# At most two row transfers in flight, and first batch of eight tiles, in a routed-experts kernel

## The reference, cut to what matters

```python
x = x + L0_ffn(L0_cond(x))
X = L1_cond(x)                                   # (64 sequences, 64, 256)
X = X + attention(rmsnorm(X, g1))                # the "block"
xf = rmsnorm(X, g2).reshape(-1, 256)             # 4096 tokens
logits = xf @ Wr.T + expert_bias                 # 8 experts
topw, topi = top_k(softmax(logits), 2)
combine = sum(one_hot(topi) * softmax(topw))
shared = swiglu(xf, sW1, sW2, sW3)
eo = einsum(silu(xf @ eW1) * (xf @ eW3), eW2)    # per expert
out = x + X + shared + sum(combine * eo)
```

## Time and profile before

| what | us |
|---|---|
| median of 3 executions | 1442.61 (1438.27 to 1443.07) |
| the profiled execution | 1443.43 |
| its span | 1441.7 |
| PE busy | 1307.1 |
| DVE busy | 1037.4 |
| ACT busy | 897.6 |
| POOL busy | 708.2 |
| the 64 row transfers, start of the first and the last | 1062.2 and 1199.9 |
| the first and the last routed tile's transpose | 1209.8 and 1393.9 |

### The profile page before, as it was taken

One profiled execution on the slowest core, in us unless ns is written; L12 is line 12 of the kernel. 1 busy time (PEld: TensorE's weight loads), 2 busy tenths in 40 slices (PEclk: granted clock), 3 DMA queues, 4 the chain that ended last, 5 costly groups with the idle time before them and its releaser, 6 DMA issues.

```text
span 1441.7 us, 42824 instructions
## 1 busy us (share of the span) xinstructions
PE 1307.1 (91%) x15311; PEld 1157.7 (80%) x15312; DVE 1037.4 (72%) x2148; ACT 897.6 (62%) x2309; POOL 708.2 (49%) x797
## 2 busy tenths in 40 slices
PE   4899999999689999889999999689999789999980
PEld 3799999998579999778888888668788678888870
DVE  4798988988736465687887887768987686555446
ACT  3677777777356666656666666478775354555545
POOL 2556555564435454545445444357777562333330
PEclk8899999999799999999999999899997999999995
DMA  8200000001030000000000000020012623333319
GB/s 230 54 8 10 8 9 9 8 11 37 3 87 1 1 0 1 3 9 10 8 9 9 9 9 12 23 56 16 16 29 72 211 80 111 105 104 101 101 44 349
DMA packets 87025, 71.19 MB, mean 49 GB/s; under 512 B 49981, under 2 KB 80831, under 8 KB 85824
## 3 DMA queue, kind: packets, MB, share of 16 engines
q1 hardware_dynamic: 80320, 51.73, 12.7%
q0 software_dynamic: 6528, 17.05, 3.3%
HBM read 39.47 MB, written 24.02 MB: 44 GB/s over the span
## 4 chain that ended last, share of the span: by engine, by line
PE 56%; issue 20%; POOL 10%; DVE 9%; ACT 3%; DMA 1%; another core or an unknown queue 0%; ACTq 0%; POOLq 0%; DVEq 0%; SPq 0%
PE psQ L2348 9%; PE psQ L1957 7%; PE psW L2035 7%; PE psW L2327 5%; POOL pn L759 5%; PE psQ L2148 3%; POOL rq L785 3%; PE psS L2148 3%; PE psW L2136 3%; PE psM L2136 3%; PE psS L2059 2%; PE psT L1986 2%; PE psT L2070 2%; PE psM L2009 2%; PE psT L2316 2%
## 5 line engine op out<-in xcount | busy, mean ns | idle before, releaser
L1957 PE MATMUL psQ<-xT,wq 128*128 128x256 f32 x1536 | 224.8, 298 | 3.5 <-ACT cur L1117 1.8
L2035 PE MATMUL psW<-wout,oT 128*128 128x256 f32 x1536 | 207.8, 294 | 1.1 <-ACT oT L980 1.1
L1957 PEld LDWEIGHTS psQ<-xT,wq 128*128 128x128 f32 x1536 | 205.0, 201 | 4.4 <-issue 2.6
L2035 PEld LDWEIGHTS psW<-wout,oT 128*128 128x128 f32 x1536 | 196.6, 199 | 1.3 <-ACT oT L980 1.3
L2348 PE MATMUL psQ<-W,exT 128*128 (+1 forms) x624 | 172.3, 412 | 0.0
L759 POOL TENSOR_TENSOR pn<-ex,rden 128x1024 f32<-128x1024 f32 x64 | 124.5, 1945 | 45.2 <-DVE rden L1440 45.2
L980 ACT ACTIVATE oT<-psT,small 128x512 fp32r<-128x512 f32 x128 | 81.1, 684 | 91.3 <-PE psT L2070 91.2
L915 POOL DMA_INDIRECT results<-result,idx x72 | 70.1, 974 | 135.3 <-ACT result L1244 131.9
L803 POOL TENSOR_TENSOR hT<-hf,hT 128x512 fp32r<-128x512 f32 x64 | 85.8, 1341 | 102.1 <-ACT hT L1113 102.0
L771 POOL TENSOR_TENSOR masked_bias<-bias_t,negmask 128x1024 f32<-128x1024 f32 x32 | 68.8, 2150 | 132.6 <-DVE ex L1408 132.6
L1367 DVE SCALAR_TENSOR_TENSOR oT<-psT,small,oT 128x512 fp32r<-128x512 f32 x128 | 90.2, 746 | 58.3 <-ACT oT L980 58.3
(11 more groups left out here) (302 smaller groups left out, 3391.6 us busy)
## 6 DMA issues: line engine op xcount, KB each, us to landing
rows<-sorted SPq DMA_DIRECT2D x72, 132.0 KB, 2.1
both<-results SPq DMA_DIRECT2D x8, 1024.0 KB, 13.7
raw_w<-W SPq DMA_DIRECT2D x27, 256.0 KB
vv<-vp SPq DMA_DIRECT2D x256, 16.0 KB, 1.8
out<-X SPq DMA_DIRECT2D x8, 512.0 KB, 8.8
X<-x SPq DMA_DIRECT2D x1, 3584.0 KB, 18.1
bvv<-v_all SPq DMA_DIRECT2D x128, 16.0 KB
sorted<-rows SPq DMA_DIRECT2D x9, 132.0 KB
```

Source lines behind the costliest of these rows:

```text
L1957: mm = nc.tensor.matmul(psQ[:, cc, h * QT:h * QT + QT], wq[w][:, k, c * P:c * P + P], xT[g % 2][u][:, k, :], start=(k == 0 and j == 0), st ...
L2035: mm = nc.tensor.matmul(psW[:, 0:D], oT[u][:, c, :], wout[w][:, c, :], start=(u == 0 and c == 0 and w == 0), stop=(u == 1 and c == CH - 1))
```

## The change

- Batches are tiles 0 to 8, 8 to 24 and 24 to 32. Each choice and the places come in two parts, which may lie in different steps: batch 0's first choice in steps -18 and -17 (block steps 18 and 19), its second in -16 and -15, its places in -12 and -11. The other batches' parts stay together, batch 1's places move from step 1 to step 2.
- Batch 0 is ranked before the output projection of tile 17. Batch 1 is ranked in expert step 1, behind the block, and waits there for the last sum into O; its ranks are read with its places in step 2.
- Row transfer n waits for transfer n - 2 to have landed (two semaphores, in turn) and for no tile. 16 instead of 14 lie in the block.

```diff
-BATCHES = ((0, 12), (12, 24), (24, TILES))
-FIRST_CHOICE, SECOND_CHOICE, PLACES = (-14, -2, 5), (-13, -1, 6), (-11, 1, 8)
-RANKED_BEFORE, RANK = (19, 31), 7
-SEND_STEP, SENT_IN_BLOCK = 26, 14
+BATCHES = ((0, 8), (8, 24), (24, TILES))
+FIRST_CHOICE, SECOND_CHOICE, PLACES = ((-18, -17), (-2, -2), (5, 5)), ((-16, -15), (-1, -1), (6, 6)), ((-12, -11), (2, 2), (8, 8))
+RANKED_BEFORE, RANK = 17, {2: 1, 7: 2}
+SEND_STEP, SENT_IN_BLOCK, IN_FLIGHT = 26, 16, 2
...
-            sp.wait_ge(sem("x_sent"), 16 * TOP_K * TILES)
+            for n in range(IN_FLIGHT):
+                sp.wait_ge(sem(f"x_sent{n}"), 16 * TOP_K * TILES // IN_FLIGHT)
...
-                                             oob_is_err=False).then_inc(sem("x_sent"), 16)
+                                             oob_is_err=False).then_inc(sem(f"x_sent{(TOP_K * t + k) % IN_FLIGHT}"), 16)
...
-                if n >= SENT_IN_BLOCK and k == 0:
-                    pool.wait_ge(sem("e_xTp"), (t - SENT_IN_BLOCK // TOP_K) * 8 // 7 + 1)
+                reach(pool, sem(f"x_sent{n % IN_FLIGHT}"), 16 * (n // IN_FLIGHT))
                 send(t, k)
...
-                    if t in RANKED_BEFORE:
-                        read_ranks(RANKED_BEFORE.index(t))
+                    if t == RANKED_BEFORE:
+                        read_ranks(0)
...
-            def choose(b, n):
+            def choose(b, n, part):
...
+                if part == 0:
+                    then(nc.vector.tensor_reduce(top_w[n][:, tiles], p, AX.X, ALU.max))
+                    then(nc.vector.tensor_tensor(left, p, wide(top_w[n], b), ALU.is_lt))
+                    then(nc.vector.scalar_tensor_tensor(left, left, float(E), index, ALU.mult, ALU.add))
+                    return
...
-            def places(b):
+            def places(b, k):
 
                 tiles = slice(*BATCHES[b])
-                if b == 2:
+                if b and k == 0:
                     read_ranks(b)
...
-                    if t - 1 in RANKED_BEFORE:
-                        pe.wait_ge(sem("r_read"), RANKED_BEFORE.index(t - 1) + 1)
-                    if t in RANKED_BEFORE:
-                        rank(RANKED_BEFORE.index(t))
+                    if t == RANKED_BEFORE + 1:
+                        pe.wait_ge(sem("r_read"), 1)
+                    if t == RANKED_BEFORE:
+                        rank(0)
...
-                if i == RANK:
-                    rank(2)
+                if i in RANK:
+                    rank(RANK[i])
...
-                if b == 2:
+                if b == 1:
+                    pe.wait_ge(sem("d_X1"), TILES)
+                elif b == 2:
                     pe.wait_ge(sem("t_olo"), 2 * BLK + TILES)
```

More of the change, by code:

```diff
@@ L1768, in choose @@
                 expert = xf_all[:, tiles, D + 1] if n == 0 else rc[0][:, tiles]
-                then(nc.vector.tensor_reduce(top_w[n][:, tiles], p, AX.X, ALU.max))
-                then(nc.vector.tensor_tensor(left, p, wide(top_w[n], b), ALU.is_lt))
-                then(nc.vector.scalar_tensor_tensor(left, left, float(E), index, ALU.mult, ALU.add))
+                if part == 0:
[3 more added lines that the diff above has]
+                    return
                 then(nc.vector.tensor_reduce(expert, left, AX.X, ALU.min))
@@ L1804, in read_ranks @@
                 dve.wait_ge(sem("r_read"), b + 1)
-            def places(b):
+            def places(b, k):
                 tiles = slice(*BATCHES[b])
-                if b == 2:
+                if b and k == 0:
                     read_ranks(b)
[L1811 to L1814, removed]
+                mine = rt[1 + k][:, tiles, :]
+                then(nc.vector.tensor_tensor(mine, mine, place_of[:, tiles, :], ALU.mult))
+                then(nc.vector.tensor_reduce(pos[:, k, tiles], mine, AX.X, ALU.add))
+                if k == 0:
+                    return
                 nc.vector.tensor_copy(row_place[:, :, tiles], pos[:, :, tiles]).then_inc(sem("r_placed"), 1)
@@ L1885, in first_half @@
             def first_half(i):
[L1886 to L1893, removed]
+                for b in range(len(BATCHES)):
+                    for part in range(2):
+                        if i == FIRST_CHOICE[b][part]:
+                            if part == 0:
+                                logits_there(b)
+                            choose(b, 0, part)
+                        if i == SECOND_CHOICE[b][part]:
+                            choose(b, 1, part)
+                        if i == PLACES[b][part]:
+                            places(b, part)
+                if i in ENDS:
                     tile_ends(ENDS.index(i))
```

## The result

| what | before | after |
|---|---|---|
| median, us | 1440.78 | 1445.68 |
| ratio | | 1.0037 [1.0024, 1.0049] |
| the profiled execution (span) | 1443.43 (1441.7) | 1446.94 (1445.2) |
| start of row transfer 16, of the last | 1118.95, 1199.86 | 1116.49, 1204.86 |
| PE through with the shared expert | at the first routed tile | about 1189.5 |

The forecast was 3.4 us faster in the profiled execution, 1440.0; it came out 3.5 us slower, 1446.9. In medians, 1439.2 was forecast and 1445.7 measured, 4.9 us slower than before. That is within the range of 1430 to 1449, but the kernel moved to the other side.

The account below looks back on a forecast made before the run. PE, busy 91% of the span, was taken as the bound, so gains had to come before the first routed tile: -5.3 + 1.9 = -3.4 us, giving 1440.0 profiled, 1439.2 in the median. The range was 1430 to 1449.

Parts of the forecast that it names:

- part 4: Row transfers, two in flight: 1.63 us apiece, plus 2.9 us beside the weights' loads; last start 1198.7, rows at 1204.4.
- start of transfer 16: Batch 1's first row transfer, once DVE has its places in expert step 2: forecast to start at 1119.2.
- 47 intervals: The transfers behind number 16: 47 x 1.63 = 76.6 us, plus 2.9 us for slower landings beside the weights' loads.
- last start to the first tile on PE: From the last row transfer's start to the first rows being there: 5.65 us, as before the change.
- clock behind the idle time: First routed tile: PE's clock at its lower level after idling makes a step 4.4 us for 2.54, +1.9 us.
- Part 1: Block: batch 0 of 8 tiles, chosen in halves, costs 2.2 us for 4.5, so -2.3 us.
- Parts 2 and 3: Batch 1 of 16 tiles costs +0.4 us, its moved rank 0; the first 16 transfers in the block cost 0.
- Part 5: Shared expert: stalls gone, PE ready at about 1194, waits for rows until 1204.4; -5.3 us at the first routed tile.
- Part 6: First routed tile: PE's clock is at its lower level after some 10 us idle, +1.9 us.
- Rival A: Row transfers: the cap's pace is too slow; at 3.0 us landing, 1.93 us apiece, 1450.3 us; chance 0.17.
- C: Row transfers: the cap does nothing, POOL prepares while waiting, pace stays 1.28 us; -15.4 us, 1427.2; chance 0.15.
- B: Shared expert: ACT's and DVE's stalls are not the transfers' doing and stay; -1.9 us, 1440.7; chance 0.18.

Follow-up runs that it names:

- e4: The changed kernel with the old release by tiles in place of the cap of two: 1422.7 us, ratio 0.9999.
- e10: Same kernel as e4, in another set: the changed kernel with the old release by tiles and no cap; 1422.3 us, ratio 0.9998.
- e12: The kernel before with the cap of two in place of its release by tiles, old batches kept: 1446.6 us, ratio 1.0180.
- e5: The changed kernel, unaltered, measured again in the set of e6 and e7: 1446.2 us, ratio 1.0025.
- e6: The changed kernel without the cap or any wait for a tile, same kernel as e3 in another set: 1475.4 us, ratio 1.0231.
- e7: The kernel before, unaltered, profiled in the set of e5 and e6: 1444.9 us, a single time.
- e3: The changed kernel without the wait for transfer n - 2 or for any tile: 1422.6 us, ratio 1.0003.
- e18: The changed kernel without the cap, with one POOL operation of 0.58 us between two transfers: 1447.7 us, ratio 1.0059.
- e19: The changed kernel, unaltered, measured again in a later set than e5: 1447.2 us, ratio 1.0049.
- e11: The changed kernel without the cap, with two one-column POOL memsets between two transfers: 1420.7 us, ratio 0.9992.
- e16: The changed kernel without the cap, with three one-column POOL memsets between two transfers: 1423.8 us, ratio 0.9999.

## Why the prediction was wrong

The failing step is part 4, the landing time beside the weights' loads. It was bounded at 2.4 and 4.0 us, by stores and by landings with little else on the DMA engines, and 2.9 us were taken for it. It came out at about 6.0 us there, for which the five intervals from 1121.45 to 1138.58 cost 17.13 - 5 x 1.63 = 9.0 us; single late landings behind it cost another 2.8. In all the 47 intervals took 88.4 us for 76.6 + 2.9. The stretch was as long as forecast (17.1 us for 18); the pace in it was 3.43 us apiece, for 2.43 at the upper bound. With 9.0 for 2.9 the forecast's own sum gives 1446.1. Two of the single late intervals (from 1146.36 and from 1164.02) have a packet of an instruction queue beside them in the DMA view, a third such packet, at 1182.6, has none; that was not followed up.

By the steps of the forecast, in the profiled execution:

| term | predicted | measured | difference |
|---|---|---|---|
| start of transfer 16 | 1119.2 | 1116.49 | -2.7 |
| 47 intervals | 79.5 | 88.4 | +8.9 |
| last start to the first tile on PE | 5.65 | 5.53 | -0.1 |
| clock behind the idle time | 1.9 | 2.9 | +1.0 |
| the sum | | | +7.1 |

The forecast and the profiled execution differ by 6.9 us (1440.0 and 1446.9). The clock's 2.9 is the time from the first routed tile to the end of the span, 234.8 us for 231.95 before.

- *Part 1* had the direction, half the size. The nine steps from 18 to 27 take 45.60 us (1013.98 to 1059.58), 3.3 over 9 x 4.70, for 4.5 before: 1.2 us won, not 2.3. e4 and e10 show that none of it reaches the end by more than the measurement can tell. Transfer 16 started earlier than forecast because the whole kernel was already 2.9 us ahead at step 18 (1013.98 for 1016.86), which the change does not touch: that is chance, and it flatters the changed kernel by as much in this one pair of executions.
- *Parts 2 and 3* cost nothing that shows, though the wait of part 3 was not free: POOL sits idle for 1.49 us before transfer 14, at the end of the block, until a landing.
- *Part 4*'s frame held: the mechanism, the 3.2 us from n to n+2, 1.62 us apiece away from the loads. The Trainium skill ("DMA: Bandwidth & Descriptors", "Latency and other measured facts"), by whose 2 us at high load a landing of 4.2 us was estimated, had the right sign and was also too short for 6.0.
- *Part 5* was right that the stalls go (PE ready at 1189.5, forecast 1194; idle time 20.9 us, forecast 10), and wrong in what it rested on. It took the stalls as a fixed part of the kernel before. They are not: where they don't occur, before takes 1422, and the same cap costs 1.8% there (e12).
- *Part 6*: 2.8 to 2.9 us for 1.9, at a granted clock of 0.50 as forecast. Two tiles run slow, not one.

Rival A is what happened, in its own terms: its break-even was an average pace of 1.77 us and it put 1450.3 (a median) at 1.93; the pace was 1.88, the median 1445.7. It had a chance of 0.17, because the median landing spoke against it. That median was of stores that run while the DMA engines' share is 0.31. C fell: away from the loads transfer n+2 starts 3.2 us behind n, not 2.6, so POOL does begin only after the landing. B fell with e5, e6 and e7: on one chip the stalls grow when the limit goes and are absent with two in flight.

What stays open: what in a chip makes ACT and DVE stand still while POOL issues back to back. The trace says "remote" and no more; traffic on the DMA engines is the same with and without (e3 and e6, 0.75 and 261 GB/s in both), and in e6 the DMA view has a single packet of an instruction queue between 1117.3 and 1192.5, at 1146.5, and none near the beginning or the end of any of the three stalls shown. That speaks against stalls that end with an instruction refill. The Trainium skill ("Runtime: NRT & Kernel Launch", "Instruction fetch mechanics"), by which a refill is mostly hidden, is not contradicted by that. Nor is it settled whether the chip itself or the occasion makes the difference, or whether three in flight would be free of stalls on such a chip, and so would win.

## What to carry to other kernels

A limit on transfers in flight is a chain: its length is their number times the landing time and the 0.86 us to the next start, over the limit, and the landing time must be taken from where the transfers will run, beside the largest loads, not from a median of quiet ones. Count how long PE can be late before that chain is what it waits for: removing the stalls in front of it, 18 us by the difference between the chips, was worth nothing, as the chain's end came at the same place. And when the bound is a stall that the trace puts down to "remote", ask for the kernel's own time on another chip, or at another time, before a saving is built on it: here one kernel took 1422 in one set and 1443 in another.

## What the runs showed of the hardware

- With back-to-back indirect DMAs issued by POOL (1.28 us apart) ACT stands still for up to 14.3 us at a time and DVE for 7.7 in one set (e6, 1475.4), and neither does in another (e3, 1422.6), with the same kernel; the cause is open.
- At a pace of 1.83 us, or with two in flight, there was none of it where the kernel before takes 1439 to 1443 (e18, e5, e19).
- An indirect DMA of 128 rows of 1056 bytes lands in about 2.4 us at a DMA share of 0.2 to 0.3 (3.2 us from n to n+2, less 0.86) and in about 6.0 us while the weights' loads hold the share at 0.99 (the changed kernel, 1121 to 1138).
- One-column memsets on POOL between two indirect DMAs cost nearly nothing: three took 0.19 us and moved the pace from 1.28 to 1.30 (e11, e16).
